# One gather of w0 by batch, table windows by gather, constants in two parts, and a place of its own for each tile's k and v rows

## The reference

```python
w = w0_table[conditions]                      # L0: a 32x32 matrix per batch, from 200
x = x + einsum('bct,bcd->bdt', x, w)
q, k, v = x @ Wq.T, x @ Wk.T, x @ Wv.T        # L1: 8 query heads, 4 kv heads of 32
q, k = rope(rms(q)), rope(rms(k))             # positions kv_lens + 0..31
# k, v are written into a paged cache (blocks of 16 positions; 257 blocks named per
# batch by block_tables, several batches may name the same block), which is then read
# back: each token sees the 128 positions up to its own
x = x + softmax(mask(q @ k_all.T)) @ v_all @ Wo.T
x = x + x @ W_base.T + lora(x, adapter)       # L2: adapter of rank 16, one of 4 per batch
x = x + einsum('bct,bcd->bdt', x, w3[subject])# L3: a 32x32 matrix per batch, from 8
```

## Time and profile before

| | us |
|---|---|
| median of 3 runs | 255.35 (254.97 to 255.81) |
| the profiled execution, its own time | 254.57 |
| its span, first to last instruction | 252.7 |
| around the span | 1.87 |
| busy: DVE / PE / ACT / POOL | 206.2 / 197.3 / 128.9 / 118.4 |

### The profile page before, as it was taken

One profiled execution on the slowest core, in us unless ns is written; L12 is line 12 of the kernel. 1 busy time (PEld: TensorE's weight loads), 2 busy tenths in 40 slices (PEclk: granted clock), 3 DMA queues, 4 the chain that ended last, 5 costly groups with the idle time before them and its releaser, 6 DMA issues.

```text
span 252.7 us, 7114 instructions
## 1 busy us (share of the span) xinstructions
PE 197.3 (78%) x2402; PEld 153.1 (61%) x2402; DVE 206.2 (82%) x542; ACT 128.9 (51%) x491; POOL 118.4 (47%) x135
## 2 busy tenths in 40 slices
PE   0060669949866776799578999999999999999981
PEld 0040557635533343598466878888888887878760
DVE  0788873794899999999859999999999989899740
ACT  0203001433544333538187788777777788766610
POOL 4265686614667666557603234555444355520010
PEclk9999985897999999999859999999999999999998
DMA  4925999603554211112501254544445454440011
GB/s 130 315 55 130 207 228 402 154 21 100 155 160 131 77 43 36 41 59 67 139 25 27 86 141 138 152 126 108 154 143 147 145 157 139 113 129 27 27 48 42
DMA packets 18868, 29.86 MB, mean 118 GB/s; under 512 B 8733, under 2 KB 14184, under 8 KB 18450
## 3 DMA queue, kind: packets, MB, share of 16 engines
q0 software_dynamic: 7408, 19.04, 27.3%
q1 hardware_dynamic: 8674, 5.30, 7.3%
q10 hardware_dynamic: 2752, 5.08, 6.4%
HBM read 29.48 MB, written 7.38 MB: 146 GB/s over the span
## 4 chain that ended last, share of the span: by engine, by line
PE 20%; DMA 14%; DVE 11%; issue 8%; ACT 1%; POOL 1%; POOLq 0%; DVEq 0%; ACTq 0%
DMA big<-in_pool,idx 12%; PE quad L1186 6%; PE bank L1172 5%; PE bank L1212 2%; DVE qrot L952 2%; DVE work L995 2%; DMA big<-merged,idx 2%; PE quad L1207 2%; DVE onT L1002 2%; PE bank L1226 1%; PE bank L1168 1%; PE bank L1200 1%; DVE late L974 1%; PE bank L1219 1%; DVE nmx L985 1%
## 5 line engine op out<-in xcount | busy, mean ns | idle before, releaser
L671 ACT ACTIVATE work<-bank,nmx 128x164 f32<-128x164 f32 x128 | 50.0, 409 | 25.8 <-DVE nmx L985 25.8
L1172 PE MATMUL bank<-kt_rope,big 128*128 128x164 f32 x256 | 45.6, 313 | 0.0
L1172 PEld LDWEIGHTS bank<-kt_rope,big 128*128 128x128 f32 x256 | 41.8, 199 | 4.4
L1141 PE MATMUL quad<-wqkv_sb,yall 128*128 128x512 f32 x64 | 34.6, 667 | 11.7 <-ACT yall L628 11.7
L535 POOL DMA_INDIRECT big<-merged,idx x16 | 16.7, 1045 | 39.0 <-DMA big<-in_pool,idx 28.5
L995 DVE STREAM_TRANSPOSE work<-work 128x768 f32<-128x768 f32 (+1 forms) x64 | 32.6, 546 | 0.0
L985 DVE TENSOR_REDUCE nmx<-bank 128x3 f32<-128x492 f32 (+1 forms) x48 | 28.3, 590 | 4.1 <-PE bank L1172 3.6
L507 POOL DMA_INDIRECT merged<-work,idx x16 | 17.4, 1089 | 23.1 <-DVE work L937 13.3
L671 ACT ACTIVATION_READ_ACCUMULATOR work<-bank,nmx 128x1 f32 x128 | 27.4, 214 | 0.0
L650 ACT ACTIVATE big<-qT,con 128x256 f32<-128x256 f32 x64 | 27.2, 500 | 0.0
L618 ACT COPY work<-quad 128x384 f32<-128x384 f32 x16 | 7.7, 479 | 37.3 <-PE quad L1141 37.3
(11 more groups left out here) (154 smaller groups left out, 408.7 us busy)
## 6 DMA issues: line engine op xcount, KB each, us to landing
merged<-big ACTq DMA_DIRECT2D x3, 1024.0 KB, 9.7
xin<-in_x SPq DMA_DIRECT2D x16, 128.0 KB, 3.3
out<-x4s SPq DMA_DIRECT2D x16, 128.0 KB, 2.3
w3bd<-w_scratch SPq DMA_DIRECT2D x64, 4.0 KB, 2.4
con<-in_consts SPq DMA_DIRECT2D x1, 676.5 KB, 5.0
wqkv_sb<-in_wqkv ACTq DMA_DIRECT2D x1, 512.0 KB, 6.1
wt_sb<-in_wt ACTq DMA_DIRECT2D x1, 256.0 KB, 7.1
wp_sb<-in_wp ACTq DMA_DIRECT2D x1, 256.0 KB, 7.4
```

What stands on the lines that cost most here:

```text
L671: act.activation(prob[:, p, hd, 0:NK], ps_sc[(p + i) % 2][:, j * NK:j * NK + NK], ACT.Exp, bias=nmx[:, p, hd:hd + 1], scale=1.0, accum_out ...
L1141: mm = pe.matmul(ps_qkv[p][:, :], x1T[:, t, c, :], wqkv_sb[:, c, :], start=(c == 0), stop=(c == 1))
L1172: mm = pe.matmul(at[:, j * NK:j * NK + NK], qbd[:, p, hd, :], kT[:, p, hd // GSZ, 0:NK], start=False, stop=(j == n - 1), skip_group_check= ...
```

## The change

- **w0.** One gather takes 64 rows of 4 KB, one for each batch, into `w0g`; POOL adds 1 on the diagonals; SP writes it to a scratch tensor in HBM and, when that has landed, reads it back in four transfers of 512 pieces of 128 bytes straight into the diagonal blocks of `w0i`, which DVE has cleared at the start. The 16 gathers and DVE's four products are gone. All 16 tiles now wait for the same event, `s_w0`.
- **Block table.** The host passes a view of the table in which row `257 b + slot` holds the eleven entries needed; DVE works out that row number in seven small steps and POOL gathers 64 rows of 44 bytes. DVE's eleven comparisons are gone.
- **Constants** are loaded in two parts: 315 columns by SP at the start, 740 by ACT behind the weights (`s_conl`). Weights signal on three semaphores in place of one.
- **Own blocks.** Blocks 0 and 2 are gathered, block 1, of which every row is overwritten or dropped, is not: its place in `merged` is filled with zeros from `own`. All three go out on SP, inside the row of x loads (after those of tiles 5, 6 and 7), and no longer on ACT.
- **Buffers.** `kqs`, `sq`, `ss` and `rt` hold four tiles; each tile has its own place for k and v rows, in `qT`, and for rotated k and q, in `big` (`rot`). ACT copies `x1T` of a tile ahead of k, q and v of the one before. Root and epsilon are one instruction. The rotated sum is one instruction in place of two.
- **Order.** `base(t)` stands inside the loop for 8 tiles, the LoRA part of the other 8 is done in two groups of four tiles. The list steps come later in the row of tiles, the outward weight products stand within it (`outward`), and scatters start at POOL's step 7, two in a step up to step 10. `zscale` and `w3e` (L789, L790, L801 before) are made between the phases. `normalised(t)` transposes into `qT`, so it waits for tile t's scatter.

```diff
+_COLS = [("ident", 128), ("m4", 36), ("m8", 24), ("m16", 48), ("seg1", OWN), ("tok", TOK), ("inv", HD // 2),
+         ("adapter", 1), ("batch", NB), ("rowtok", 1), ("place", NB), ("tile", NT), ("eps", 1), ("halfpi", 1),
+         ("later", OWN * B * OWN), ("backpos", NKB), ("ownpos", 2 * Q2)]
+FIRST = 14
...
-        w0_f = sb("w0_f", [128, NT])
         w0i = sb("w0i", [128, NT, 128])
+        w0g = yall[0:B, NT - 4:NT, :].rearrange("p t n -> p (t n)")
...
-        kqs = carve(2, 384)
-        sq = carve(2, 384)
+        kqs = carve(RING, 384)
+        sq = carve(RING, 384)
...
-        rsum = carve(2, 128)
-        kvrow = carve(RING, ROW)
-        ss = carve(2, 12)
...
-        stage = big[0:B, :].rearrange("p (j n) -> p j n", j=OWN)
+        rot = big[:, 0:384 * NT].rearrange("p (t n) -> p t n", t=NT)
+        kvrow = qT
+        stage = big[0:B, 4096:12288].rearrange("p (j n) -> p j n", j=2)
...
-        INLINE = 4
+        INLINE = 8
...
+        SCATTER = {s: () for s in range(7)}
+        SCATTER.update({7: (0, 1), 8: (2, 3), 9: (4, 5), 10: (6, 7), 11: (8,)})
+        SCATTER.update({s: (s - 3,) for s in range(12, NT + 3)})
...
-            sp.dma_start(kv_i, kv_lens).then_inc(s_small, 16)
-            sp.dma_start(tab_i, table_i).then_inc(s_small, 16)
-            sp.dma_start(con[:, :], consts).then_inc(s_con, 16)
-            sp.dma_start(row_i[:, :, :].rearrange("p k t -> p (k t)"), of_rows).then_inc(s_rowi, 16)
...
+            sp.dma_start(ids_i, ids).then_inc(s_ids, 16)
+            sp.dma_start(con[:, 0:NEARLY], consts[:, 0:NEARLY]).then_inc(s_con, 16)
...
+            for r in range(2):
+                sp.dma_start(xin[:, r, :], x[128 * r:128 * r + 128, :]).then_inc(s_x[r], 16)
...
+            sp.wait_ge(w0g_done, 1)
+            sp.dma_start(w0_d, w0g).then_inc(s_w0d, 16)
+            sp.wait_ge(s_w0d, 16)
+            sp.wait_ge(w0_blank, 1)
+            for b in range(NB):
+                sp.dma_start(w0i[32 * b:32 * b + 32, :, 32 * b:32 * b + 32],
+                             w0_d.rearrange("(t b) (c d) -> b c t d", b=NB, c=TOK)[b]).then_inc(s_w0, 16)
...
+            def old_rows(i):
+
+                sp.wait_ge(s_stage[i], 16)
+                sp.dma_start(merged_blocks[2 * B * i:2 * B * i + B, :], stage[:, i, :]).then_inc(s_init, 16)
...
+                if s == 7:
+                    sp.wait_ge(s_big, 1)
+                    sp.dma_start(merged[B * BLOCK:2 * B * BLOCK, :].rearrange("(p f) n -> p f n", p=128),
+                                 own[:, :, :].rearrange("p r (f n) -> p (r f) n", n=ROW)).then_inc(s_init, 16)
...
-            def l0_weights(t):
-
+            wait(s_ids, 16)
+            pl.indirect_dma_start(
+                out=w0g, out_offset=None, in_=w0_rows,
+                in_offset=bass.IndirectOffsetOnAxis(ap=ids_i[:, 1:2], axis=0),
+                bounds_check=w0_rows.shape[0] - 1, oob_is_err=False, engine_sem=desc_w0).then_inc(s_w0g, 16)
+            wait(s_win, 1)
+            pl.indirect_dma_start(
+                out=blk_i[:, :], out_offset=None, in_=windows,
+                in_offset=bass.IndirectOffsetOnAxis(ap=win_i, axis=0),
+                bounds_check=windows.shape[0] - 1, oob_is_err=False, engine_sem=desc_w0).then_inc(s_tab, 16)
+
+
+            wait(s_w0g, 16)
+            diagonal = bass.AP(w0g.tensor, w0g.offset, [w0g.ap[0], (TOK + 1, TOK)])
+            pl.tensor_scalar(diagonal, diagonal, 1.0, None, ALU.add).then_inc(w0g_done, 1)
...
+            wait(s_tab, 16)
+            for i, j in enumerate((0, 2)):
...
-            wait(s_w0i, 1)
-            for t in range(0, 6):
-                l0_weights(t)
...
-            for j in range(OWN):
-                pl.indirect_dma_start(
...
+            def scattered(t):
+
+                if t == 0:
+                    wait(s_rows, 1)
+                    wait(s_init, 48)
...
+                    in_=kvrow[:, t, :], in_offset=None,
+                    bounds_check=SEGS * BLOCK - 1, oob_is_err=False, engine_sem=desc_scat).then_inc(s_scat[t], 16)
...
+            for s in range(NT + 3):
+                if s < NT:
+                    rotated(s)
+                if s == 2:
+                    pl.memset(own[:, :, :], 0.0).then_inc(s_big, 1)
+                for t in SCATTER[s]:
+                    scattered(t)
+                    if t < RING:
+                        cached(t, t)
...
-            for j in range(OWN):
-                act.wait_ge(s_stage[j], 16)
-                act.dma_start(merged_blocks[B * j:B * j + B, :], stage[:, j, :]).then_inc(s_init, 16)
...
+            def outward():
+
+                act.wait_ge(s_out2, 1)
+                act.copy(aow[:, :, 0:E * R], ps_pre[:, 384:512].rearrange("p (c n) -> p c n", c=2)).then_inc(s_prec, 1)
+                act.copy(wob[:, :, :], ps_wob[:, :].rearrange("p (c n) -> p c n", c=2)).then_inc(s_prec, 1)
+                act.activation(identb[:, :], ident, ACT.Copy, scale=NEG).then_inc(s_ident, 1)
...
-                t, k, p, r, n = at_step4(h, u, 2)
-                if valid(t):
-                    act.wait_ge(qkv_done, t + 1)
...
-                    act.copy(kqs[:, p, :], ps_qkv[p][:, 0:384]).then_inc(kq_copied, 1)
...
                 t, k, p, r, n = at_step4(h, u, 1)
                 if valid(t):
                     act.wait_ge(xT_done, t + 1)
                     act.copy(x1T[:, t], ps_xT[p][:, 0:256].rearrange("p (c n) -> p c n", c=2)
                              ).then_inc(xT_copied, 1)
...
+                if valid(t):
+                    act.wait_ge(qkv_done, t + 1)
+                    if t >= RING:
+                        act.wait_ge(prods_done, t - 3)
+                        act.wait_ge(cross_done, 2 * (t - 3))
+                    act.copy(kqs[:, r, :], ps_qkv[p][:, 0:384]).then_inc(kq_copied, 1)
...
+                t, k, p, r, n = at_step4(h, u, 4)
...
+            ve.memset(w0i[:, :, :], 0.0).then_inc(w0_blank, 1)
...
+            link(ve.tensor_tensor(win, slot0, basef, ALU.add))
+            ve.tensor_copy(win_i, win).then_inc(s_win, 1)
...
-            AFTER = {0: same_blocks, 1: segments, 2: lists_of_rows, 3: shifted_lists, 4: rows_of_tiles}
...
+            AFTER = {0: segments, 2: lists_of_rows, 3: shifted_lists, 4: rows_of_tiles}
+
+            same_blocks()
+
+            def phase1(t):
...
-                            ve.wait_ge(kT_part, t + 1)
-                            ve.tensor_scalar(ss[:, p, :], ss[:, p, :], 1.0 / HD, EPS, ALU.mult, ALU.add
-                                             ).then_inc(ss_done, 1)
...
-                                      (G, 12, qT[:, t, :].rearrange("p (n a d) -> p a n d", a=2, d=half))):
-                        ve.tensor_tensor(dst,
-                                         ropeA[:, p, :].rearrange("p (a n d) -> p a n d", a=2, d=half)[:, :, a:b, :],
-                                         ropeB[:, p, :].rearrange("p (a n d) -> p a n d", a=2, d=half)[:, :, a:b, :],
-                                         ALU.add).then_inc(qraw_done if a else rsum_done, 1)
+                    ve.tensor_tensor(rot[:, t, :].rearrange("p (n a d) -> p a n d", a=2, d=half),
+                                     ropeA[:, p, :].rearrange("p (a n d) -> p a n d", a=2, d=half),
+                                     ropeB[:, p, :].rearrange("p (a n d) -> p a n d", a=2, d=half),
+                                     ALU.add).then_inc(rsum_done, 1)
...
+                    ve.tensor_tensor(kvrow[:, t, 0:128].rearrange("p (n d) -> p n d", n=G),
+                                     rot[:, t, 0:128].rearrange("p (n d) -> p n d", n=G),
+                                     rinv[:, t, 0:G].unsqueeze(2).broadcast_to([128, G, HD]),
...
+            ve.wait_ge(s_num, 32)
+            link(ve.tensor_copy(adp_f[:, :], adp_i[:, :]))
+            link(ve.tensor_scalar(zscale[:, :], adp_f[:, :], cc("adapter", E * R), scal[:, 0:1],
+                                  ALU.is_equal, ALU.mult))
+            ve.wait_ge(s_w3e, 16)
+            ve.tensor_tensor(w3e[:, :, :], w3e[:, :, :], cc("ident", TOK)[:, 0:TOK].unsqueeze(1)
+                             .broadcast_to([TOK, 8, TOK]), ALU.add).then_inc(w3e_done, 1)
...
+                ve.wait_ge(s_scat[t], 16)
...
-            pe.wait_ge(s_wb, 2)
...
+            def outward():
+
+                pe.wait_ge(s_wb, 2)
+                pe.wait_ge(y_copied, 2)
+                pe.wait_ge(zx_copied, 2)
...
+            def adapters(g):
+
...
                 for c in range(2):
-                    mm = pe.matmul(ps_y[t % 2][:, D:D + 128], aw[:, c, :], x1T[:, t, c, :],
+                    mm = pe.matmul(ps_zx[g % 2][:, :], aw[:, c, :], x1T[:, 4 * g:4 * g + 4, c, :],
...
-            INDEX = {1: dead_tokens, 2: canonical, 4: tiles}
...
+            INDEX = {3: dead_tokens, 4: canonical, 5: outward, 7: tiles}
...
-                    pe.wait_ge(w0i_done, 1 if t < 4 else 2 if t < 7 else 4)
+                    pe.wait_ge(s_w0, 16 * NB)
```

400 lines of the change are left out of this document (182 added, 218 removed).

## The result

The kernel after takes 259.59 us, median of 4 runs (259.01 to 262.49), against 255.58 (254.97 to 256.46, 4 runs) for the kernel before on the same chip: a ratio of 1.0165, 95% interval 1.0107 to 1.0223. It is slower by 4 us, where 245.0 was predicted. The profiled execution took 259.99, its span is 258.0. (Several kernels here have executions more than 1.5% above their quickest one; ratios leave these out, medians and ranges don't, and e7 and e9 have too few others for a ratio.)

What follows compares the result with a forecast made beforehand. It took ACT's 16.8 us setup wait, then nearly level DVE and PE, then DVE's chain as bounds. Keys of tile 0 at 111.8 for 122.15, 10.4 less, made 254.57 into 244.2; 0.8 for the median gave 245.0, range 239 to 252.

Steps and rivals of the forecast that it cites:

- When w0 is there: Setup: ids, gather, SP's write and four reads bring w0 at 20 us, or 17 if pieces flow during issue.
- the price of 27 ns a piece: Reads of w0: 2048 pieces of 128 bytes at 27 ns each over 16 engines, 3.5 us.
- the rival "slower": Setup: w0's pieces pass only behind the own-block gathers, w0 at 31.8, 256.5 us; slower or about equal has 0.09.
- the 42.6% of the earlier trace: Share of 16 engines' 1.5 us taken by 382 small packets; source of the 27 ns a piece for w0's reads.
- What bounds the kernel now: Setup: ACT's 16.8 us wait for the third own block; then DVE and PE nearly level, then DVE's chain alone.
- From w0 to the lists and tile 7: First phase: from w0 at 20, lists end at 51.9, k and q of tile 7 at 65.0.
- POOL's row of scatters: First phase: first scatter behind tile 7's rope product at 65.0, step 11's product ends 85.4, last k row 98.5.
- Between the phases: Last k row to keys of tile 0: 0.95 for moved instructions plus 12.33 as before, keys at 111.8.
- The second phase: From the keys of tile 0 to the end: not edited, stays 130.55 us.
- The five terms: The forecast's stretches: w0's arrival, w0 to tile 7, POOL's scatters, between the phases, second phase; 244.2 us for the profiled execution.

Runs made afterwards that it cites:

- e7: e1 with ACT's eight loads of weights and constants issued only when the gather of w0 has landed; 252.24 us.
- e9: The edits of e5, e6 and e7 together, on e1; 248.25 us (243.37 to 251.04), no ratio.
- e1: Kernel after, with POOL issuing the two own-block gathers only when the reads of w0 have landed; 252.59 us, ratio to before 0.987.
- e3: Kernel before, with the three sends of own blocks to merged moved from ACT to SP's row; 255.69 us, ratio 1.000.
- e6: e1 with DVE's zscale and w3e sums behind the segments step and one semaphore for scatters of tiles 0 to 11; 254.18 us, ratio 0.987.
- e12: e10 with 8 unused TensorE products ahead of the wait for the lists; 241.27 us, ratio to before 0.944.
- e10: e9 with DVE's mask products moved to where the lists are ready and POOL's prob memsets behind two pairs of fetches; 245.61 us, ratio 0.958.
- e5: e1 with scatters earlier, one each behind rope products of tiles 5 to 8, then two at 9 and 10; 249.94 us, ratio 0.976.
- e11: e10 with 17 unused TensorE products ahead of the wait for the lists; 246.27 us, ratio to before 0.957.
- e14: e1 with unused TensorE products, 14 ahead of the wait for w0 and 8 ahead of that for the lists; 249.25 us, ratio 0.975.

## Why the prediction was wrong

**When w0 is there: the step that failed.** 20 was forecast, 31.8 came. The sum had no wait of the reads behind the own-block gathers, and what stands ahead of the reads was sized too small. Up to SP's write it is 5.5 us late: ids 4.08 for 2.8 (+1.3), the gather 8.55 for 4.8 (+3.7), the write 3.4 for 2.9. With the weights held back (e7) ids take 1.93 and the gather 5.20, so the weights beside them are the whole of the first and 3.3 of the second. The reads took 13.7 from that landing in place of 7.7: 4.6 when nothing is in their way (e1), so the price of 27 ns a piece was more than twice what e1 shows (12.6), and 9.1 of waiting behind 2 MB of own blocks, which was put at nothing.

That is the rival "slower", with its mechanism and nearly its time (256.5; the rest is below). That its place is right to the digit, 31.8, is luck: it had the gathers landed at 28.3 and 3.5 for the pieces behind them; the second one landed near 30.9 (14.1 after its issue at 16.8) and the last read 0.9 later. The rival had 0.09. Its argument against, that reads and gathers are on different queues, didn't hold here: q1 moved 6 packets in 7 us while q0 had work. It was also priced as a rare case, though the prediction's own times put the gathers (to 13) right ahead of the reads (from 12.6). And the prediction didn't see that `allblk` goes the same way.

In one sentence the prediction reads the 42.6% of the earlier trace rows as "nearly a third"; its sum uses 42.6%. That small pieces are a loss is borne out: they move 9.7 bytes in a ns of one engine in e1, the larger ones of the earlier trace rows 15.6.

**What bounds the kernel now.** The bound was read wrong as well: ACT's 16.8 us were taken as real time because they were the longest wait. e3 shows 0.07 us behind them at the first k, q, v and 0.35 at the keys. The list steps in TensorE's row, with DVE's `same_blocks` at 35.9, were late next, and the prediction named no such step. The forecast didn't rest on it, since it built the new order up from w0, but its trust in a gain did.

**From w0 to the lists and tile 7.** 45.0 forecast, 45.5 measured: right in the kernel after. In part by luck: with w0 at 21.8 (e1) it took 48.1, since TensorE was slower (the first k, q, v 3.62 for 2.68, the list step 2.74 for 1.58), and with fillers in its waits 43.7.

**POOL's row of scatters.** The steps came as described (6.3 for a double step with its product, forecast 6.2; POOL not idle for 28 us), but from tile 7's rope product to the last k row it took 35.3, not 33.5. Of this, 1.2 came by the end of tile 11's product, where scatters took 1.18 to 1.36 in place of 1.1 in steps 8 to 11, and 0.6 behind it, where DVE's L945 took up to 1.83. That DVE and POOL held each other up there fits these rows; no run tested it alone. The first scatter was where the prediction put it, behind tile 7's rope product.

**Between the phases.** 13.3 forecast, 14.3 measured. The moved sums cost 1.06 (forecast 0.95); the rest, 0.9, goes with the second wait ahead of each transpose (a turn of product and transpose is 0.86 in place of 0.79, 12 times), which was put at nothing. e6 takes both back but for 0.4.

**The second phase.** 130.55 forecast, 131.0 measured.

The five terms are 12.0 + 0.5 + 1.8 + 1.0 + 0.5 = 15.8 us: 244.2 and 15.8 is 260.0, the profiled execution's 259.99. Against the kernel before the change lost 5.4 in that execution; e1 says that without the queueing it would have won 1.6 (252.99 against 254.57 in the profiled executions, 1.3% by the ratio), and e12 that 5.6% is there with the gathers, weights, scatters, masks and TensorE's idle time in other places. How much of that is the new layout isn't shown: the late weights and the fillers were not tried on the kernel before, where TensorE waits 3.38 ahead of its list step and then takes 3.35 for k, q, v as well.

## What to carry to other kernels

Before many engines' work is hung on one small transfer, list every large transfer that is issued ahead of it on any queue, and add their bytes: here each MB cost it 5 us. The longest wait in the profile is worth only what is left when the next wait in the same rows takes over; undo it alone before building on it. And where TensorE waits some microseconds, look at its products behind the wait: here they could take 2.7 for 1.5 and 3.5 for 2.0. Unused products inside such a wait gave some of that back; those that ran beyond it gave nothing.

## What the runs showed of the hardware

- A large gather on POOL's software queue holds up small pieces of the hardware queues, and SP in issuing them (4.27 us for an issue that takes 0.56 without the gather): q0 had 92.7% of 16 engines' time and q1 0.1% over 7 us; where they took turns it was 13 pieces of 128 bytes for 13 rows of 16 KB in 1 us, and alone 932 pieces in 1 us.
- Pieces of 128 bytes cost 12.6 ns of one engine each in e1 (2537 packets, 122 bytes on average) and 20 ns in the fullest microsecond of the kernel after (932), against 27 ns for the mixed packets of the earlier trace rows.
- A scatter that POOL begins 0.3 us behind the start of two DVE products of two SBUF tensors each takes 2.79 us (e6) and 2.80 (e9) in place of 0.98 (before, e1, e10).
- TensorE's granted clock was 0.50 to 0.53 behind waits of 4 us (e1, e5, e10) and 1.00 behind the same stretch filled with products (e11, e14); the list step took 2.74 and 1.51. In e9 the list step was still quick behind the same wait, and the k, q, v slow. Behind 33 products of one column the clock was 0.55 (after, 46 to 49.4).
- With the weights' loads in the DMA engines a load of 0.8 KB took 4.04 us in place of 1.93, and a gather of 256 KB 8.11 in place of 5.20 (e1, e7).
